# Routed FFN by sorted tokens: attention of all batches first, then nine one-expert tiles read back from memory; causal masks of the scores on TensorE, row maxima straight from PSUM

## The reference, cut to what matters

```python
mod = (_silu(c) @ wmod).reshape(16, 6, 1, -1)          # shifts, scales and gates sa ca ga sb cb gb, per batch
ga = (2 * (ga >= 0) - 1) * jnp.maximum(jnp.abs(ga), 0.25)   # gb likewise
h = _layernorm(x) * (1 + ca) + sa
q = h @ w_dq.T @ w_uq.T;  kv = h @ w_dkv.T @ w_ukv.T    # 16 heads of 16
attn = softmax(q k^T / 4 + causal mask)                 # 256 x 256 per head
x = x + ga * ((attn @ v) @ w_out.T)
h = _layernorm(x) * (1 + cb) + sb
top_expert = argmax(softmax(h @ Wg.T))                  # 2 experts
out0 = gelu(h @ W0a.T + b0a) @ W0b.T + b0b              # 256 -> 512 -> 256
out1 = relu(h @ W1a.T + b1a) @ W1b.T + b1b
x = x + gb * (out0 where expert 0, out1 where expert 1)
```

## Time and profile before

| | |
|---|---|
| Time, median of 3 runs | 595.14 us (594.93 to 599.59) |
| The profiled execution's own time | 593.84 us |
| Its span (first to last instruction) | 592.1 us |
| PE matmuls busy | 515.4 us, 87% of the span |
| DVE busy | 480.8 us, 81% |
| ACT busy | 366.5 us, 62% |
| POOL busy | 311.9 us, 53% |
| DMA queue q1 | 43.19 MB, 39.1% of the 16 engines' span |

### The profile page before, as it was taken

How to read it: one execution, slowest core, us unless ns; L and a number is a source line. 1 busy time by engine, 2 the same in 40 slices (tenths; PEclk the granted TensorE clock), 3 DMA queues, 4 the chain that set the end, 5 groups by cost and what they waited for, 6 DMA issues and landing times.

```text
span 592.1 us, 14257 instructions
## 1 busy us (share of the span) xinstructions
PE 515.4 (87%) x4912; PEld 446.2 (75%) x4912; DVE 480.8 (81%) x949; ACT 366.5 (62%) x521; POOL 311.9 (53%) x300
## 2 busy tenths in 40 slices
PE   4534685989999999999999999999999999999974
PEld 4424463788888988888888888788988898888874
DVE  3538163779999899989898989999899999887573
ACT  1524464858585866667676858585766667676320
POOL 6235232455656665755646565656665665552441
PEclk9856598899999999999999999999999999999998
DMA  8835453262707080716244351708080615210100
GB/s 246 206 46 76 50 74 75 52 95 37 128 18 145 2 161 3 121 42 90 71 68 93 50 111 31 130 7 154 0 152 13 108 39 91 55 39 2 37 19 18
DMA packets 43802, 43.74 MB, mean 74 GB/s; under 512 B 5344, under 2 KB 40800, under 8 KB 43760
## 3 DMA queue, kind: packets, MB, share of 16 engines
q1 hardware_dynamic: 43760, 43.19, 39.1%
HBM read 13.39 MB, written 4.23 MB: 30 GB/s over the span
## 4 chain that ended last, share of the span: by engine, by line
PE 49%; DVE 19%; DMA 10%; issue 9%; SPq 5%; POOL 3%; ACT 3%; DVEq 0%; POOLq 0%; ACTq 0%
DMA qs<-parts_q 8%; PE ps_s L382 6%; DVE mx L933 6%; PE ps_t L401 5%; PE ps_o L419 3%; PE ps_a L333 3%; PE ps_t L405 3%; SPq L282 3%; PE ps_a L334 3%; PE ps_a L335 3%; PE ps_c L333 3%; PE ps_c L335 2%; PE ps_c L334 2%; PE ps_o L333 2%; POOL xs L1186 2%
## 5 line engine op out<-in xcount | busy, mean ns | idle before, releaser
L794 ACT ACTIVATE score_rows<-ps_s 128x1024 f32<-128x1024 f32 x96 | 98.8, 1030 | 79.3 <-PE ps_s L382 66.2
L1246 POOL TENSOR_SCALAR_AFFINE_SELECT score_rows<-score_rows 128x512 f32<-128x512 f32 (+1 forms) x96 | 80.0, 834 | 110.4 <-ACT score_rows L794 109.8
L933 DVE TENSOR_REDUCE mx<-score_rows 128x4 f32<-128x1024 f32 (+1 forms) x96 | 114.6, 1210 | 5.7 <-POOL score_rows L1246 5.5
L806 ACT ACTIVATE p<-ps_t 128x1024 f32<-128x1024 f32 x96 | 98.5, 1026 | 17.9 <-PE ps_t L405 17.3
L382 PE MATMUL ps_s<-ks,qs 96*128 96x256 bf16 (+1 forms) x512 | 63.3, 260 | 33.2 <-DMA qs<-parts_q 29.7
L382 PEld LDWEIGHTS ps_s<-ks,qs 96*128 96x128 bf16 x512 | 37.0, 103 | 47.9 <-DMA qs<-parts_q 23.2
L1186 POOL TENSOR_TENSOR xs<-z,xs 128x512 f32<-128x512 f32 (+1 forms) x16 | 34.9, 2182 | 68.7 <-DVE z L1022 68.7
L401 PE MATMUL ps_t<-qs,ks 99*128 99x256 bf16 (+1 forms) x512 | 61.1, 254 | 11.0 <-DMA qs<-mx_rows 10.3
L401 PEld LDWEIGHTS ps_t<-qs,ks 99*128 99x128 bf16 x512 | 38.8, 101 | 17.5 <-DMA qs<-mx_rows 6.3
L405 PE MATMUL ps_t<-past_b,ident_b 128*128 128x256 bf16 (+1 forms) x192 | 46.0, 322 | 0.0
L1234 POOL TENSOR_TENSOR hid_lo<-hid,hid_hi 128x512 fp32r<-128x512 f32 x32 | 42.8, 1350 | 4.8 <-DVE hid_hi L1092 4.8
(11 more groups left out here) (166 smaller groups left out, 1631.4 us busy)
## 6 DMA issues: line engine op xcount, KB each, us to landing
qs<-parts_q SPq DMA_DIRECT2D x96, 128.0 KB, 4.0
ks<-parts_k SPq DMA_DIRECT2D x96, 128.0 KB, 4.7
xs<-x SPq DMA_DIRECT2D x16, 256.0 KB, 4.1
gates<-gates_scratch SPq DMA_DIRECT2D x16, 256.0 KB, 4.5
out<-xs SPq DMA_DIRECT2D x16, 256.0 KB, 2.9
p<-wmod SPq DMA_DIRECT2D x1, 1024.0 KB, 6.7
p<-waT SPq DMA_DIRECT2D x1, 1024.0 KB, 9.1
p<-wmod SPq DMA_DIRECT2D x1, 512.0 KB, 5.9
```

What stands on the lines that cost most here:

```text
L794: act.activation(score_rows[c % 2][:], ps_s[:], ACT.Copy).then_inc(scores_out, 1)
L806: act.activation((p0, p1)[tile][:, h0:h0 + n, :], ps_t[:].rearrange("p (h s) -> p h s", h=n), ACT.Exp, scale=SCALE).then_inc(exp_done, 1)
L933: dve.tensor_reduce(dst, score_rows[c % 2][:].rearrange("p (h k) -> p h k", h=n), AX_X, ALU.max).then_inc(max_done, 1)
L1246: pool.affine_select(out=diag, in_=diag, compare_op=ALU.is_ge, fill=NEG, base=0, pattern=[[0, n], [-1, P]], channel_multiplier=1).then_inc ...
```

## The change

The kernel is rewritten in two parts. **Attention of all batches**: 21 steps (`LAGS = 5`, 16 batches), now written out without a loop. Input norm at lag 0, projections at lag 1, scores and maxima at lag 2, exponentials and values at lag 3, output projection, second norm and the choice of the expert at lag 4, and at lag 5 the token's place in the sorted order and its row's DMA. The stacks and `v` have three buffers. **Scores**: the causal mask is added in PSUM by two more matmuls per chunk (`masked`, a bf16 identity times `future_b`), DVE takes the maxima from `ps_s`, and `scores_copy`, `hide_scores` and `score_rows` are gone. PE's next chunk waits for `max_done` where it waited for `scores_out`. `h_high`, `q_second` and `k_second` go from DVE to ACT. **Sorting**: the choice is a sum over x times the difference of the two gate rows (`choose_expert`, a multiply with a running sum, twice a batch, and four operations on 1 or 2 columns); a matmul with a triangle of ones gives each token's rank (`rank`, `place`), and POOL writes rows of 769 floats (modulated input, x, the last gate, the token's number) to the scratch `sorted_scratch` in DRAM by an indirect DMA for each 128 tokens (`put_rows`). Tokens of expert 0 fill it from the front, those of expert 1 from the end. SP fills the gates' part of each row by broadcast DMAs. Near the end six more indirect DMAs fill the gap.

**Tiles**: 9 tiles of 512 tokens follow, of one expert each. SP loads a tile (128 x 4 x 769 floats, 1.57 MB) into one of two buffers, PE turns it (`turn_tile`), `up` takes 24 matmuls of 512 columns, `down` 48 of 256. ACT and DVE copy the expert's weights for each tile, ACT makes the gelu with the expert's arguments and the high parts, DVE the relu's maximum, the low parts and the bias, POOL multiplies by the gate and adds x (`finish_half`) and writes the rows to `out` by four indirect DMAs (`put_half`).

The core of the diff:

```diff
-        LAGS = 4
...
+        LAGS = 5
...
+        def pipeline(step):
+
+            for s in range(NB + LAGS):
+                step(lambda lag: Batch(s - lag, NB))
...
-            def stack(b, part, side, parts, stacks, ready, done):
-
-                if b.off:
-                    return
-                wait(sp, st_done, CH * (b.n - 1))
...
+            def stack(b, part, side, parts, stacked, ready, done):
+
+                if b.off:
+                    return
+                wait(sp, st_done, CH * (b.n - 2))
                 wait_alone(sp)
...
+            def load_tile(i):
+
+                if i >= NT:
+                    return
+                wait(sp, out_stored, 16 * TJ * (i - 1))
+                sp.dma_start(tile_rows[i % 2], sorted_dram[i * TS:(i + 1) * TS, :].rearrange("(j p) w -> p j w", p=P)
+                             ).then_inc(tile_in[i % 2], 16)
+
             for n in range(2):
-                sp.wait_ge(stored[n], 16 * NB // 2)
+                sp.wait_ge(put[n], 16 * NB)
+            for i in range(NT):
+                load_tile(i)
+            sp.wait_ge(out_stored, 16 * TJ * NT)
...
-                wait(pe, scores_out, CH * b.n + c)
+                    pe.wait_ge(mod_rows_ready, 5)
+
+                wait(pe, max_done, CH * b.n + c)
                 tile, heads = (0, range(8 * c, 8 * c + 8)) if c < 2 else (1, range(4 * c - 8, 4 * c - 4))
                 width = P * (tile + 1)
+                a_bank = 512 // width
                 for n, h in enumerate(heads):
-                    mm = pe.matmul(ps_s[:, n * width:(n + 1) * width], qs[b.parity][0:R, h, tile * P:(tile + 1) * P],
-                                   ks[b.parity][0:R, h, 0:width], start=True, stop=True)
+                    pe.matmul(ps_s[:, n * width:(n + 1) * width], qs[b.third][0:R, h, tile * P:(tile + 1) * P],
+                              ks[b.third][0:R, h, 0:width], start=n % a_bank == 0, stop=False)
+                for bank in range(2):
+                    mm = masked(ps_s[:, bank * 512:(bank + 1) * 512], a_bank, width - P, future_b)
...
+            def turn_tile(i):
+
+                if i >= NT:
+                    return
+                pe.wait_ge(tile_in[i % 2], 16 * (i // 2 + 1))
+                for k in range(KT):
+                    for j in range(TJ):
+                        mm = pe.transpose(ps_t[:, k * TS + j * P:k * TS + (j + 1) * P], tile_rows[i % 2][:, j, k * P:(k + 1) * P], ident[:])
+                mm.then_inc(tg_done, 1)
...
+            turn_tile(0)
+            for i in range(NT):
+                up(i)
+                turn_tile(i + 1)
+                down(i)
...
             def row_max(b, c):
                 if b.off:
                     return
-                dve.wait_ge(scores_hidden, CH * b.n + c + 1)
+                dve.wait_ge(s_done, CH * b.n + c + 1)
...
-                dve.tensor_reduce(dst, score_rows[c % 2][:].rearrange("p (h k) -> p h k", h=n), AX_X, ALU.max).then_inc(max_done, 1)
+                dve.tensor_reduce(dst, ps_s[:].rearrange("p (h k) -> p h k", h=n), AX_X, ALU.max).then_inc(max_done, 1)
...
+            def put_rows(b):
+
+                if b.off:
+                    return
+                pool.wait_ge(pos_ready, b.n + 1)
+                pool.wait_ge(g_ready, b.n + 1)
+                pool.wait_ge(number_ready, b.n + 1)
+                pool.wait_ge(last_in[b.pair], 32 * (b.turn + 1))
+                pool.wait_ge(x1_ready, b.n + 1)
+                if b.n == NB - 1:
...
-                pool.tensor_tensor(rows, y[:], rows, ALU.add).then_inc(out_ready, 1)
+                    pool.indirect_dma_start(sorted_dram, bass.IndirectOffsetOnAxis(ap=pos[b.pair][:, t:t + 1], axis=0),
+                                            comb[b.pair][:, t, :], None).then_inc(put[b.pair], 16)
...
+            def finish_half(i, q):
+
+                some = tile_rows[i % 2][:, 2 * q:2 * q + 2, :]
+                pool.wait_ge(y_ready, 2 * i + q + 1)
+                pool.tensor_tensor(some[:, :, 0:D], some[:, :, 0:D], some[:, :, 2 * D:3 * D], ALU.mult).then_inc(y_gated, 1)
+                pool.wait_ge(y_gated, 2 * i + q + 1)
+                pool.tensor_tensor(some[:, :, 0:D], some[:, :, 0:D], some[:, :, D:2 * D], ALU.add).then_inc(out_ready, 1)
+
+            def put_half(i, q):
+
+                pool.wait_ge(out_ready, 2 * i + q + 1)
+                pool.wait_ge(row_of_ready, i + 1)
+                for j in range(2 * q, 2 * q + 2):
+                    pool.indirect_dma_start(out_rows, bass.IndirectOffsetOnAxis(ap=row_of[i % 2][:, j:j + 1], axis=0),
+                                            tile_rows[i % 2][:, j, 0:D], None, bounds_check=TOKENS - 1, oob_is_err=False
+                                            ).then_inc(out_stored, 16)
+
+            for i in range(NT):
+                finish_half(i, 0)
+                put_half(i, 0)
+                finish_half(i, 1)
+                put_half(i, 1)
 
```

## The result

| | before | after |
|---|---|---|
| Time, median | 595.92 us (594.93 to 599.59, 4 runs) | 745.69 us (744.4 to 748.76, 4 runs) |
| The profiled execution's span | 592.1 us | 742.7 us |
| PE busy | 515.4 us | 492.8 us |
| DVE busy | 480.8 us | 450.4 us |

The changed kernel takes 1.2507 times as long as the one before, 95% interval 1.2438 to 1.2575. Every engine is busy for less time and the whole is slower: the time is in waits. The forecast was 715 us, 640 to 790.

The account below looks back on a forecast made before the run. PE and DVE, both full, were taken to bound the kernel before. Attention's start 102, steps 270 and 45, end 43, tiles 253 and 1.7 outside the span sum to 714.7, about 715 us; range 640 to 790.

Parts of the forecast that it names:

- The ring: Tiles: PE's and SP's orders close a loop of down, bias, POOL, stores, load and turning; 29 us, counted seven times.
- The step: Attention: one pipeline step takes 24.5 us, from DVE's work plus waits for PE and POOL.
- DVE's list: Attention step: DVE's work after removals and additions, 20.6 us.
- The score buffer's 2.0 of waits: Attention step: single `ps_s` makes PE and DVE alternate; DVE loses 0.4 twice and 1.2 between maxima.
- DVE waits 1.3 for `comb`: Attention step: second norm's statistics wait for POOL's add, behind two indirect DMAs; 1.3 us lost.
- `h_low` holds back `compress` for 0.6 more: Attention step: `h_low`, late on POOL behind the add, delays PE's `compress` by a further 0.6 us.
- The rest of attention: Attention outside steps 5 to 15: start 102 us, steps 16 and 17 45, step 18 13, steps 19 and 20 30.
- The indirect DMA: POOL, attention steps and tiles: each indirect DMA assumed to cost 1.2 us, without a trace row for it.
- B: Rival, whole kernel: indirect DMA 0.3 us, load 5, tile loop 22, attention step 22.6; 641 us, chance 0.14.
- C: Rival, whole kernel: indirect DMA 2.4 us, POOL and DVE block each other, step 27.5, loop 36; 802 us, chance 0.12.
- D: Rival, attention: PE's pauses lower its clock; 839 us at low clock throughout, 777 more likely; chance 0.05.
- E: Rival, tiles: loop not felt, tiles 11.5 us apart; 567 us with steps of 22.6; chance 0.09.

Follow-up runs that it names:

- e1b: Changed kernel with PE's turning of the next tile behind this tile's down, and DVE's bias ahead of the next tile's low parts and target rows: 681.5 us.
- e2b: Changed kernel with a third tile buffer, PE's and DVE's orders kept: 639.9 us.
- e12: Changed kernel with four tile buffers, attention-step orders on POOL and SP rearranged, and DVE's expert choice one step later: 569.5 us, 0.958 of the time before.
- e1: Changed kernel with only PE's tile order altered, turning of the next tile behind this tile's down: 728.0 us.
- e3: Changed kernel with POOL making `h_low` ahead of the second norm's power instead of behind it: 729.9 us.

## Why the prediction was right, and where its steps were not

The total came out 30.7 us above the forecast, inside the range, with the sign right. The sum was 714.7; the profiled execution took 744.4, 21.9 more in attention (481.85 in place of 460) and 7.9 more in the tiles.

**The ring: right in mechanism and in sum.** Foretold 29, measured 29.46 a tile. Bias 0.4, measured 0.8; POOL's operations and indirect DMAs 10.2 together, measured 11.4 (537.23 to 548.66), the term that was most short: 0.8 us ahead of each pair of DMAs were not in it, and L1434 takes 1.62 us beside DVE's copies and low parts, 1.27 in e1b; landing 2.5 and 2.44; load 7 and 6.42; turning 2.0 and 1.97; `down` 7.0 and 6.7. By the Trainium skill, "DMA: Bandwidth & Descriptors" (Anatomy of one DMA), the load was estimated at 5.6 us. The page fits DMAs issued from GpSimd, and this load is issued by SyncE, which the prediction left unsaid; the trace has 6.4, and the measurement stands. That the ring is in the program's order and not in durations is shown by e1b, e2b and e12: the same work at 19.4, 14.5 and 13.0 us a tile. One thing it got wrong without paying for it: it named PE's and SP's orders as what closes the ring, and DVE's closes it too (e1). Ahead of the ring 26.1 us against 25.5; behind it 28.5 against 24.4, since tile 8 comes 13.1 us after tile 7 and the last halves and stores take 15.4.

**The step: right in size (24.5 against 25.2), wrong in its parts.** PE's 19.6 is right (19.7 at full clock in e3). DVE's list was too long: 20.6 us were foretold, and it is busy 20.9 only because POOL holds it for 2.6 of them (cast 1.6, modulation 1.0), which leaves an estimate of some 18.3. The score buffer's 2.0 of waits are 2.8, and 1.0 of waiting for ACT's first part of q, behind PE at half clock, wasn't in the sum. The step that failed is the last: "DVE waits 1.3 for `comb`" and "`h_low` holds back `compress` for 0.6 more". DVE hardly waits for `comb`, since its cast is held until POOL's add has ended, 1.6 us, the same delay under another name. And `h_low` holds `compress` back 2.2: I had walked POOL's list to `h_low` and left out that the power ahead of it waits for DVE's statistics behind the cast. What I had given no time at all is the clock: 1.8 us a step. So 24.5 was reached from DVE's side with a list too long, and 25.2 came about on PE's side by pauses and a low clock that the sum didn't have; that the number came so close was luck.

**The rest of attention.** Against the sum: 8.8 us for eleven steps (278.8 in place of 270, by the adds), 2 for steps 16 and 17, 8.1 in step 18 (21.1 in place of 13, where the six exponentials also wait until the last batch's maxima have come in), 5.8 in steps 19 and 20; 3 came back, because the adds count from 99.0 and not 102.

**The indirect DMA: right.** 1.2 was assumed from POOL's nearest rows; it takes 1.0 us and the next starts 1.3 to 1.4 after it (1.5 behind the third of most tiles, which takes 1.2).

**The rivals.** B and C fall by that same row. C's blocking is real but small in the ring, 0.7 us on POOL's two adds; in a step it is 2.6 us of DVE's time, 1.6 in the cast, which lies on the path, and 1.0 in the modulation. D was given 0.05 and a test, a granted clock well under 1 between 120 and 370 us; the clock is 0.90 there. It is D's mechanism at a fifth of its price (1.8 us a step, where the low clock throughout was 34 in place of 24.5), and D should have been a term of the sum and not a rival for the whole: the row that showed the clock low while the pipeline filled was there. E's point of decision, a ring under 14 us, holds: in e12 the ring allows a tile each 29.5 / 3 = 9.8 us, and with it the kernel is faster than before. That its 569.5 us lie near E's 567 is luck: E had tiles of 11.5 and steps of 22.6, e12 has 13.0 and, by orders that E did not have, 21.0.

**Signs named.** PE idle 10 us or more ahead of each turning: 15.0 to 15.6 in the ring. Indirect DMAs 1.2 apart: 1.3, in most tiles once 1.5. PE some 80% busy in the steps: 85%. DVE waiting for `comb`: missing.

## What to carry to other kernels

When two engines' lists, a load and a store close a ring, the ring's length over the number of tiles that one turn carries is the time of one tile, as long as that is more than the busiest engine's own work. With the orders kept a turn carries one tile less than there are buffers, since the next tile is turned ahead of this one's `down`: one of 29.5 us with two buffers, two at 14.5 with three, three at 9.8 with four, where PE's work takes over at 13. With both orders opened, two buffers carry two (38 to 40 us, 19.4 a tile). Count this before cutting work, and look for every list that closes the ring: opening the first of two (e1) gave 18 of the 64 us that both gave. A third buffer was worth 106 us here, and the whole change turned from 25% slower to 4% faster by buffers and by the order of a few calls. An instruction that is moved behind another inherits every wait ahead of it in that queue (`h_low` behind a power behind DVE's statistics; the stacks behind a fetch behind an indirect DMA), and this is read from the list of waits, not from busy times.

## What the runs showed of the hardware that I had not expected

- A cast on DVE of 32 columns takes 0.18 us by itself, 1.80 when POOL's add of 512 columns comes beside it, and 3.01 when two such POOL operations follow each other without a gap; it ends with the last of them. The add's recorded start is 0.48 us behind the cast's, later than the cast alone would have ended, so the start of the hold can't be read from the two rows. In the step at 403, where the cast is through in time (403.16, 0.18 us, beside an indirect DMA's issue), the subtraction behind it is held until the add has ended (L1105, 1.81 in place of 0.19). The maxima, read from PSUM, are not slowed (1.22 us). The Trainium skill, "SBUF — State Buffer" (Who interferes with whom), has casts among the operations that can take the pair of ports shared with GpSimd, and reductions not: the rows agree. It has the one wait for the other's instruction; in e3 the wait lasted through two.
- PE's clock fell to half with two pauses of 1.5 and 2.2 us that were 1.2 us of work apart, in every full step from 131 to 383 us, and came back 2.9 to 6.2 us after PE had started again. In e3 a pause of 2.7 us, followed some 5 us of work later by pauses of 0.5 and 0.9, left it at 1.00.
- An indirect DMA of 128 rows costs POOL 1.0 us and 0.3 until the next starts, whether its rows are 3 KB (L1353) or 1 KB (L1441) long, and in the tiles there are 0.8 us between POOL's own last result and the first of a pair. The first of a tile's second pair takes 1.2 in most tiles.
